# Router softmax of a fused Mamba + mixture-of-experts kernel: one exponential of a difference instead of two biased ones, and two small router steps given to VectorE

## The reference

```python
logits = jnp.tanh(xt @ Wg1.T) @ Wg2.T          # (tokens, 8)
_, top_idx = jax.lax.top_k(logits, 2)
top_logits = jnp.take_along_axis(logits, top_idx, axis=1)
top_scores = jax.nn.softmax(top_logits, axis=1)
scores = jnp.zeros_like(logits).at[rows, top_idx].set(top_scores)
up = jnp.einsum('td,ehd->teh', xt, Wup) + bup
h = jax.nn.silu(up)
down = jnp.einsum('teh,eoh->teo', h, Wdown) + bdown
out = jnp.einsum('te,teo->to', scores, down)
```

## Time and profile before

| | us |
|---|---|
| runs (3) | 1413.3, 1411.35, 1413.16 |
| median | 1413.16 |
| the profiled execution, whole | 1413.3 |
| its span from first to last instruction | 1411.4 |
| PE busy | 1329.5 (94%) |
| DVE busy | 1223.3 (87%) |
| POOL busy | 1138.8 (81%) |
| ACT busy | 986.5 (70%) |

### The profile page before, as it was taken

The page is one execution under the profiler, slowest core; times in us unless marked ns, Lnnn a source line. Parts: engine busy times, 40 slices in busy tenths (PEclk is TensorE's granted clock), DMA queues, the critical chain, the costliest instruction groups (busy, mean ns, idle before and its releaser), DMA issues. The chain is left out here.

```text
span 1411.4 us, 23410 instructions
## 1 busy us (share of the span) xinstructions
PE 1329.5 (94%) x7500; PEld 957.1 (68%) x7500; DVE 1223.3 (87%) x1725; ACT 986.5 (70%) x2076; POOL 1138.8 (81%) x1173
## 2 busy tenths in 40 slices
PE   8888777999999999999999999999999999999998
PEld 3455645677766776677766776677766767778897
DVE  4899999889897899789997899789997999897564
ACT  4865787488956797488856797488857776656654
POOL 1699889789996989889996989789996978874332
PEclk9899767999999999999999999999999999999999
DMA  6441212235342442435242432435342333433342
GB/s 207 165 151 59 54 46 89 73 96 173 89 133 86 145 123 91 135 103 160 89 136 83 150 120 92 141 104 150 89 135 86 118 119 112 133 91 107 125 129 72
DMA packets 99266, 160.91 MB, mean 114 GB/s; under 512 B 9261, under 2 KB 33965, under 8 KB 99145
## 3 DMA queue, kind: packets, MB, share of 16 engines
q1 hardware_dynamic: 99144, 159.42, 36.6%
HBM read 150.60 MB, written 8.79 MB: 113 GB/s over the span
## 5 line engine op out<-in xcount | busy, mean ns | idle before, releaser
L791 POOL TENSOR_TENSOR DB<-DU,BR 128x512 f32<-128x512 f32 x448 | 579.8, 1309 | 45.7 <-DVE H L1205 24.1
L1230 DVE SCALAR_TENSOR_TENSOR ACC<-pb,CTM,ACC 128x512 f32<-128x512 f32 x512 | 374.7, 732 | 57.5 <-PE pb L1426 56.2
L1505 PE MATMUL pb<-WD,G 128*128 128x512 f32 x856 | 405.1, 593 | 0.0
L991 ACT ACTIVATE pb<-DELP,AN 128x512 f32<-128x512 f32 x448 | 307.1, 686 | 128.4 <-DVE H L1205 126.6
L1426 PEld LDWEIGHTS pb<-ID,H 128*128 128x128 f32 x2048 | 248.3, 145 | 150.8 <-issue 97.7
L1426 PE MATMUL pb<-ID,H 128*128 128x128 f32 x2048 | 317.9, 282 | 29.2 <-DVE ACC L1230 24.5
L1475 PE MATMUL pb<-H2H,WUH 128*128 128x256 f32 x1024 | 315.0, 308 | 12.2 <-DVE TY L1279 11.9
L1205 DVE TENSOR_TENSOR_SCAN H<-pb,DB 128x512 f32<-128x512 f32 x256 | 309.6, 1210 | 15.0 <-ACT pb L991 12.2
L814 POOL TENSOR_TENSOR G<-TY 128x256 f32<-128x256 f32 x256 | 192.3, 755 | 144.5 <-DVE TY L1279 100.4
L1477 PE MATMUL pb<-H2H,WUL 128*128 128x256 f32 x1024 | 290.2, 283 | 0.0
L1476 PE MATMUL pb<-H2L,WUH 128*128 128x256 f32 x1024 | 290.0, 283 | 0.0
(11 more groups left out here) (199 smaller groups left out, 1677.7 us busy)
## 6 DMA issues: line engine op xcount, KB each, us to landing
WD<-in_wdT SPq DMA_DIRECT2D x128, 512.0 KB, 5.0
BR<-bscr SPq DMA_DIRECT2D x112, 256.0 KB, 3.9
SR<-sscr SPq DMA_DIRECT2D x128, 128.0 KB, 4.2
DU<-in_x SPq DMA_DIRECT2D x8, 1024.0 KB, 6.6
ACC<-in_x SPq DMA_DIRECT2D x16, 512.0 KB, 3.8
out<-ACC SPq DMA_DIRECT2D x32, 256.0 KB, 2.1
BR<-bscr SPq DMA_DIRECT2D x32, 128.0 KB, 3.1
DU<-in_xpT SPq DMA_DIRECT2D x8, 320.0 KB, 3.1
```

The costliest lines, as they stand in the source:

```text
L791: eng.tensor_tensor(DB[:, i % NDB], DU[:, c % 2, r], BR[:, n % 2], ALU.mult).then_inc(S["dbu"], 1)
L991: eng.activation(DA[i % NDA][:], DEL[:, c % 2, r], ACT.Exp, scale=AN[:, r, n:n + 1]).then_inc(S["da"], 1)
L1230: eng.scalar_tensor_tensor(out=acc, in0=banks[bank_of["flip", c, n, r]][:], scalar=1.0 if n < 0 else CTM[:, c % 2, j, st:st + 1], in1=acc, ...
L1505: eng.matmul(DN[j][:], G[:, (cs * NM + m) % NG, j * 128:j * 128 + 128], WD[:, (cs * NE + m // 2) % NWD, m % 2], start=False, stop=m == NM ...
```

## The change

It rewrites `e1` and moves `r4`:

- DVE gets a new instruction in `r31`, ahead of the MAX_INDEX: DM = m1 - m0 for both token tiles (tensor_tensor, 128x2). RS has four rows of two; the row that held P0 now holds DM.
- ACT's `e1` is one exponential of DM (128x2) instead of two of 128x1 and one 1 + x of 128x2.
- DVE gets `r40`: P1 = 1 + PE1 (tensor_scalar, 128x2), and the reciprocal works in place.
- `r4`, the cast of the indices, goes from POOL to DVE.
- All of these count on one semaphore `rt`, now 9 per block instead of 6; `p0` and `ixf` are gone.
- `r4` and `r40` have half-slot numbers of their own in `ROUTER`; the other numbers are the same.

```diff
@@ ROUTER, "even" @@
-             "r31": 33, "e1": 35, "r4": 38, "r41": 35, "r42": 38, "sel1": 39, "sel2": 39, "r5": 40,
+             "r31": 33, "e1": 35, "r4": 33, "r40": 34, "r41": 35, "r42": 38, "sel1": 39, "sel2": 39, "r5": 40,
...
-        PE1, P0, P1, P2 = [RS[:, i] for i in range(4)]
+        DM, PE1, P1, P2 = [RS[:, i] for i in range(4)]
...
@@ GpSimd @@
-                elif what == "r4":
-                    cs = k[0]
-                    eng.wait_ge(S["rt"], 6 * cs + 4)
-                    eng.tensor_copy(IXF[:], IX[:]).then_inc(S["ixf"], 1)
...
@@ ScalarE, e1 @@
-                    eng.wait_ge(S["rt"], 6 * cs + 2)
-                    for j in range(2):
-                        eng.activation(PE1[:, j:j + 1], MX[:, j, 0:1], ACT.Exp, scale=-1.0,
-                                       bias=MX[:, j, 1:2]).then_inc(S["e1"], 1)
-                    eng.wait_ge(S["e1"], 2 * (cs + 1))
-                    eng.activation(P0, PE1, ACT.Copy, bias=1.0).then_inc(S["p0"], 1)
+                    eng.wait_ge(S["rt"], 9 * cs + 3)
+                    eng.activation(PE1, DM, ACT.Exp).then_inc(S["e1"], 1)
...
@@ VectorE @@
                 elif what == "r31":
                     cs = k[0]
-                    eng.wait_ge(S["rt"], 6 * cs + 2)
-                    if cs:
-                        eng.wait_ge(S["ixf"], cs)
+                    eng.wait_ge(S["rt"], 9 * cs + 2)
+                    eng.tensor_tensor(DM, MX[:, :, 1], MX[:, :, 0], ALU.subtract).then_inc(S["rt"], 1)
                     for j in range(2):
                         eng.max_index(IX[:, j], MX[:, j], LG[:, j]).then_inc(S["rt"], 1)
+                elif what == "r4":
+                    cs = k[0]
+                    eng.wait_ge(S["rt"], 9 * cs + 5)
+                    eng.tensor_copy(IXF[:], IX[:]).then_inc(S["rt"], 1)
+                elif what == "r40":
+                    cs = k[0]
+                    eng.wait_ge(S["e1"], cs + 1)
+                    eng.tensor_scalar(P1, PE1, 1.0, None, ALU.add).then_inc(S["rt"], 1)
                 elif what == "r41":
-                    eng.wait_ge(S["p0"], k[0] + 1)
-                    eng.reciprocal(P1, P0).then_inc(S["rt"], 1)
+                    eng.wait_ge(S["rt"], 9 * k[0] + 7)
+                    eng.reciprocal(P1, P1).then_inc(S["rt"], 1)
```

More of the change, by code:

```diff
@@ L69 @@
              "fev": (48, 52), "hh": 61, "hl": (65, 74), "r1": 82, "r12": 84, "r2": 89, "r22": 91, "r3": 94,
-             "r31": 96, "e1": 97, "r4": 100, "r41": 98, "r42": 99, "sel1": 101, "sel2": 101, "r5": 101,
+             "r31": 96, "e1": 97, "r4": 96, "r40": 98, "r41": 98, "r42": 99, "sel1": 101, "sel2": 101, "r5": 101,
              "r52": 104, "sw": 104},
@@ L73 @@
              "fev": (46, 49), "hh": 58, "hl": (57, 70), "r1": 81, "r12": 86, "r2": 89, "r22": 84, "r3": 96,
-             "r31": 96, "e1": 97, "r4": 99, "r41": 100, "r42": 100, "sel1": 103, "sel2": 103, "r5": 107,
+             "r31": 96, "e1": 97, "r4": 98, "r40": 100, "r41": 100, "r42": 100, "sel1": 103, "sel2": 103, "r5": 107,
              "r52": 106, "sw": 106},
@@ L77 @@
              "fev": (47, 50), "hh": 55, "hl": (52, 60), "r1": 55, "r12": 56, "r2": 60, "r22": 61, "r3": 66,
-             "r31": 66, "e1": 67, "r4": 69, "r41": 71, "r42": 74, "sel1": 70, "sel2": 76, "r5": 79,
+             "r31": 66, "e1": 67, "r4": 69, "r40": 69, "r41": 71, "r42": 74, "sel1": 70, "sel2": 76, "r5": 79,
              "r52": 79, "sw": 79},
@@ L81 @@
              "fev": (-34, -30), "hh": -23, "hl": (-25, -22), "r1": -24, "r12": -23, "r2": -20, "r22": -20, "r3": -19,
-             "r31": -18, "e1": -16, "r4": -16, "r41": -15, "r42": -14, "sel1": -14, "sel2": -14,
+             "r31": -18, "e1": -16, "r4": -17, "r40": -15, "r41": -15, "r42": -14, "sel1": -14, "sel2": -14,
              "r5": -9, "r52": -10, "sw": -8}}
@@ L435, in adaln_kernel @@
                      "du", "ud", "ug", "da", "dbu", "scan", "st", "flip", "acc", "asm", "ang", "asq", "fsm", "fng", "fsq", "frs", "fxn", "ftr", "fev",
-                     "hh", "hl", "g1", "tg", "g2", "lg", "rt", "sel", "bdz", "bdh", "bdl", "e1", "p0", "ixf", "r5", "stt", "up", "th", "ys", "t1", "g", "bm",
+                     "hh", "hl", "g1", "tg", "g2", "lg", "rt", "sel", "bdz", "bdh", "bdl", "e1", "r5", "stt", "up", "th", "ys", "t1", "g", "bm",
                      "dn0", "dn1", "to", "fin",
@@ L533, in select @@
                     eng.wait_ge(S["r5"], cs)
-                eng.wait_ge(S["ixf"], cs + 1)
-                eng.wait_ge(S["rt"], 6 * cs + 5)
+                eng.wait_ge(S["rt"], 9 * cs + 8)
                 for j in range(2):
@@ L539, in select @@
             else:
-                eng.wait_ge(S["rt"], 6 * cs + 6)
+                eng.wait_ge(S["rt"], 9 * cs + 9)
                 for j in range(2):
```

## The result

| | before | changed kernel |
|---|---|---|
| median of 6 runs, us | 1412.26 | 1421.76 |
| lowest to highest, us | 1409.84 to 1413.3 | 1417.25 to 1424.52 |
| profiled execution, whole / span, us | 1413.3 / 1411.4 | 1423.3 / 1421.5 |

The ratio is 1.0068, 95% interval [1.0047, 1.0089]: the change makes the kernel slower by 9.6 us [6.6, 12.6]. I had forecast 1416.2, range 1412.3 to 1421: the direction was right, the rise of 2.9 us was under a third of what came, and the time lies above the range.

A forecast was written before the change was run, and what follows sets the result against it. PE was taken as all but full in steady state, waiting for DVE in block 0's router. Terms 1.9 - 0.5 + 0.5 + 0.95 = 2.9 us on 1413.3 gave 1416.2 us, range 1412.3 to 1421.

The forecast's parts named there:

- Which instructions POOL holds: On DVE, SBUF tensor_tensor, tensor_scalar and probably the cast wait for POOL's two-input instruction to end; reciprocal and scan do not.
- Rivals A: Only DM is held by POOL, the cast and 1 + x are not: +1.5 us, 1414.8 us; chance 0.17.
- B: Nothing is held for long, as the new instructions shift DVE and POOL against each other: 1413 us; chance 0.12.
- C: Faster: ACT's saved 0.45 us is carried to the next place where DVE and PE wait for ACT: 1410 us; chance 0.07.
- Block 0, +1.9: At block 0's router DM and the cast wait for POOL, making DVE 1.9 us late, with PE waiting throughout.
- Even blocks, net 0: Blocks 2 to 12: DVE's addition 1.4 us late, 1.0 reaching PE at worst, absorbed by its 1.69 us POOL wait: 0.
- the -0.5: Behind even routers, blocks 2 to 10: POOL loses its cast, shortening five PE waits by 0.1 us each: -0.5 us.
- Block 12, 0: Block 12 was covered by the even-block estimate worked out at block 4: net 0 us.
- rival D: 1 + x misses POOL's gap: block 0 costs 3.1 us, five POOL-bound places +1.0 each: 1423 us; chance 0.20.
- Block 13, +0.5: At block 13 the cast waits 1.25 us for POOL; partly absorbed ahead of PE's next up: +0.5 us.
- Block 14, +0.95: At block 14 DM and the cast wait for POOL, P2 gives 1.0 us back, the weight load is late: +0.95 us.
- Odd blocks and ACT: Odd blocks: holds of about 1.25 us eat DVE's 0.83 us idle time: 0; ACT loses some 0.45 us per block.

The follow-up runs named there:

- two kernels that control each other: The whole change in blocks 12 to 15 only, and in blocks 0 to 11 only, each against the kernel before: 1418.09 us (+7.3) and 1415.17 us (+4.9).
- idle twin: DM's stand-in where the kernel before got three idle DVE instructions per block, in the new steps' places and forms, on an unread tile: 1419.63 us, +9.3.

## Why the prediction came out right in direction and too small

*Which instructions POOL holds.* Right: tensor_tensor, tensor_scalar and the cast, to the end of a POOL instruction; the reciprocal not. Rivals A and B are wrong by the records of the three new instructions, C by the result.

*Block 0, +1.9.* Right: 2.07 us between the two kernels that differ there. Against the trace of before it looks like less (0.9 us at the first `up`), because in that trace block 0 itself runs 1.1 to 2.6 us later than in the kernel that has the same code there.

*Even blocks, net 0.* This step failed: the 1.0 us of lateness that is left reaches PE, and PE's 1.69 us wait for POOL takes it up. The wait did take up its 1.7 us. The matmul of the earlier trace rows that waited 1.69 us has no wait ahead of it in the changed kernel:

```profile
558.76 1.02 PE L1386 MATMUL pb<-U,DU 128*32 128x512 f32 x2
```

But what used it up was another lateness, 1.65 us at the second `up` of block 4 and of block 8, where two sums of the convolution between the first and the second `up` took 1.30 and 1.80 us instead of 0.74 and 0.72. At block 4 that was nearly all, and from the third `up` on PE is only 0.4 us later than ahead of the block. At block 8 the sum ahead of the first `up` was held as well (1.84 us): PE came 1.6 us later there, nothing was left to take it up, and 1.5 us stay; in other kernels so at block 4 too. The term counted DVE's lateness once, at the router, and left out that a shift of 1 us moves DVE's sums of the convolution into POOL's run. The reading of the waits was also too generous: only the two behind blocks 4 and 8 are 1.69 us; those behind blocks 2, 6 and 10 are 0.8, and they are 0.8 in the changed kernel too, so nothing shows the -0.5. The two kernels that control each other put blocks 1 to 11 at about 4.7 us, 0.9 of it the DMA wait above, where I had -0.5 for the even and 0 for the odd ones.

*Block 12, 0.* Wrong: 2.3 us. I had worked out block 4 and let it stand for all. In the last chunk the scan is two halves, 1.38 us instead of 1.27, and 1 + x came 0.1 us too late for the gap, which is rival D's reason:

```profile
1161.60 1.38 DVE L1201 TENSOR_TENSOR_SCAN H<-pb,ST,DB 128x256 f32<-128x256 f32 x2
1162.90 1.28 DVE L1247 TENSOR_SCALAR RS<-RS 128x2 f32<-128x2 f32 x1
...
1162.86 2.53 POOL L789 TENSOR_TENSOR DB<-DU,BR 128x512 f32<-128x512 f32 x2
```

It was issued 0.04 us behind the start of POOL's next instruction. And behind it PE has no wait for a convolution sum of POOL that could give it back.

*Block 13, +0.5.* This step failed too, and by the most in any one block: 3.8 us. I costed the cast (1.25 us; it took 1.11) and put DM at nothing, without a reason. It stands in a gapless run of POOL, ahead of a `ys`, and took 3.58; the experiment that keeps DM alone puts it at 2.2 us.

*Block 14, +0.95.* Too small: 2.0 us. P2 did give back its 1.0 us, but 1 + x missed its gap there too (1.30).

*Odd blocks and ACT.* DM 0.56 or 0.62 and the cast 0.38 us at each, inside the bounds; ACT's shorter step brought nothing that can be seen.

Blocks 12 to 14 are 8.1 us in these traces, where I had 1.45. So rival D's number was near mostly by luck: it had 1 + x miss the gap at block 0 and at five early blocks, and 1 + x missed it at blocks 12 and 14 alone.

## What to carry to other kernels

Where another engine's instruction can hold up a tiny one, the form of the tiny one is worth more than the number: eight 128x1 steps with one SBUF tensor cost nothing here, three of 128x2 and 128x16 cost over 9 us. A delay must be followed past the place where it arises to every instruction of a held form behind it, since a shift of 1 us can turn a 0.7 us instruction into a 1.8 us one far from the edit. And one worked block does not stand for all: the term must be made again wherever the neighbours' lengths differ, above all where no wait is left that takes a delay up.

## What the runs showed of the hardware that I had not expected

- A small DVE instruction that waits for POOL does not always get in at the next boundary between two POOL instructions. DM at block 13 let two pass (3.55 to 3.58 us in four kernels, issued 0.20 to 0.22 us behind the start of POOL's run), while its idle twin, issued 0.24 us behind the start of the same run, took 1.07 us. Both stand behind the wait for the two MAX; DM reads what they wrote, the twin a tile that nobody writes. What makes the difference was not tried and stays open.
- The time of a reciprocal grew with its elements: 1.09 us for 128x150 and 1.45 us for 128x208, 6.2 ns an element per partition between them, against 0.17 us for 128x2.
- Two kernels with the same code up to a place can differ by a step of 1.5 us at one `up`. The trace of before has one at its third `up` (251 us), the kernel with the change in blocks 12 to 15 alone does not, and neither do most of the others; a sum of the convolution 10 us earlier took 1.78 us in the first and 0.73 us in the second. What tips it was not tried.
